# One core, eight blocks: the first FFN of blocks 1 and 2 moved ahead of the attention projections of blocks 0 and 1

## What is computed

```python
x = x + 0.5 * ffn(layernorm(x))             # FFN "1"
x = x + attn(layernorm(x))                  # "A", and within it the gated MLP, "L"
x = x + 0.5 * ffn(layernorm(x))             # FFN "2", same weights as FFN "1"

def ffn(x):   # 8 experts that share wi and wo; each has its own LoRA of rank 4
    top1 = argmax(x @ gate_W.T + gate_b)
    inter = relu(x @ wi_W.T + wi_b + lora[top1](x))        # 256 -> 1024
    return inter @ wo_W.T + wo_b                           # 1024 -> 256

def attn(x):  # 16 heads of 16
    h = rmsnorm(x) * ln1
    q, k, v = h @ wq, h @ wk, h @ wv
    i, f = exp(clip(h @ wi + bi)), sigmoid(h @ wf + bf)
    # state along the 1024 tokens: C = f*C + i * v k^T, n = f*n + i*k ; y = C q / max(|n q|, 1)
    x = x + y @ wo
    h2 = rmsnorm(x) * ln2
    return x + (silu(h2 @ w_gate) * (h2 @ w_up)) @ w_down  # 256 -> 704 -> 256
```

## Time and profile before

| | us |
|---|---|
| median of 3 runs | 936.71 (932.42 to 938.03) |
| span of the profiled execution | 936.9 |
| TensorE busy | 865.0 (92%) |
| VectorE busy | 627.0 (67%) |
| ScalarE busy | 359.0 (38%) |
| GpSimd busy | 244.5 (26%) |
| first FFN matmul of block 0 | 20.06 |
| first gate matmul of block 0's "L" | 175.19 |

### The profile page before, as it was taken

One profiled execution on the slowest core, in us unless ns is written; L12 is line 12 of the kernel. 1 busy time (PEld: TensorE's weight loads), 2 busy tenths in 40 slices (PEclk: granted clock), 3 DMA queues, 4 the chain that ended last, 5 costly groups with the idle time before them and its releaser, 6 DMA issues. The chain is left out here.

```text
span 936.9 us, 30800 instructions
## 1 busy us (share of the span) xinstructions
PE 865.0 (92%) x12744; PEld 823.7 (88%) x12744; DVE 627.0 (67%) x1502; ACT 359.0 (38%) x716; POOL 244.5 (26%) x234
## 2 busy tenths in 40 slices
PE   2958889999899998999899999999989989898998
PEld 2947869999799998999899998999979979898998
DVE  5445677585866858486676758677576787687642
ACT  4453152433533344243523436234343452233431
POOL 2013332320422313322322313332042234411110
PEclk9988999999999999999999999999999999999999
DMA  9105434212243202442133312431035035500000
GB/s 263 57 14 140 131 95 126 66 40 70 83 132 86 58 19 55 124 126 58 36 94 116 87 40 73 139 112 35 24 103 154 11 110 140 152 25 2 1 24 23
DMA packets 66313, 76.04 MB, mean 81 GB/s; under 512 B 12702, under 2 KB 48670, under 8 KB 66176
## 3 DMA queue, kind: packets, MB, share of 16 engines
q1 hardware_dynamic: 66176, 74.09, 28.2%
HBM read 56.75 MB, written 17.30 MB: 79 GB/s over the span
## 5 line engine op out<-in xcount | busy, mean ns | idle before, releaser
L644 ACT ACTIVATE r_h<-bank 128x512 fp32r<-128x512 f32 x128 | 76.5, 598 | 233.6 <-PE bank L1128 164.9
L1093 PE MATMUL bank<-xT_hi,wi_hi 128*128 128x256 f32 x512 | 148.1, 289 | 2.6 <-DVE r_l L836 1.8
L1093 PE MATMUL bank<-wo_hi,r_h 128*128 128x256 f32 x512 | 147.7, 288 | 1.1 <-DVE r_l L836 0.5
L1095 PE MATMUL bank<-xT_lo,wi_hi 128*128 128x256 f32 x512 | 144.1, 282 | 0.0
L1094 PE MATMUL bank<-xT_hi,wi_lo 128*128 128x256 f32 x512 | 144.1, 281 | 0.0
L1095 PE MATMUL bank<-wo_lo,r_h 128*128 128x256 f32 x512 | 143.7, 281 | 0.0
L1094 PE MATMUL bank<-wo_hi,r_l 128*128 128x256 f32 x512 | 143.7, 281 | 0.0
L836 DVE SCALAR_TENSOR_TENSOR r_l<-bank,r_h 128x512 fp32r<-128x512 f32 x128 | 87.9, 687 | 82.7 <-ACT r_h L644 82.1
L1093 PE MATMUL bank<-xT_hi,wgu_hi 128*128 128x256 f32 x352 | 103.1, 293 | 0.6 <-DVE gm L845 0.5
L1093 PEld LDWEIGHTS bank<-xT_hi,wi_hi 128*128 128x128 f32 x512 | 97.3, 190 | 5.0 <-DVE r_l L836 2.4
L1093 PEld LDWEIGHTS bank<-wo_hi,r_h 128*128 128x128 f32 x512 | 96.4, 188 | 3.9 <-issue 2.5
(11 more groups left out here) (157 smaller groups left out, 2143.9 us busy)
## 6 DMA issues: line engine op xcount, KB each, us to landing
dm<-f_scratch SPq DMA_DIRECT2D x128, 128.0 KB, 3.0
arena<-parts_scratch SPq DMA_DIRECT2D x96, 128.0 KB
arena<-parts_scratch SPq DMA_DIRECT2D x96, 64.0 KB
arena<-parts_scratch SPq DMA_DIRECT2D x32, 192.0 KB
x<-in_x SPq DMA_DIRECT2D x16, 256.0 KB, 3.0
parts_scratch<-pa SPq DMA_DIRECT2D x64, 64.0 KB
parts_scratch<-pb SPq DMA_DIRECT2D x64, 64.0 KB
parts_scratch<-pc SPq DMA_DIRECT2D x64, 64.0 KB
```

The source lines that it names most:

```text
L644: nc.scalar.activation(flat(r_h[:, n]), U[use % 2][:], ACT.Relu).then_inc(f_rh, 1)
L1093: nc.tensor.matmul(dst, lh, rh, start=first, stop=False, **more)
L1095: return nc.tensor.matmul(dst, lh, rl, start=False, stop=last, **more)
```

## The change

In the head of the run list two pairs change places: block 1's first FFN stands ahead of block 0's attention, block 2's ahead of block 1's. The rest of the list is the same. All five order strings are replaced, for the whole length of the program. No function changes.

```diff
-RUNS = [("1", 0), ("A", 0), ("1", 1), ("A", 1), ("1", 2)]
+RUNS = [("1", 0), ("1", 1), ("A", 0), ("1", 2), ("A", 1)]
...
 ORDER = {
     "PE": """
-        3G U G 5U V 2U V 2U 2V 4U V U V U 2V 2G 5U G U G 2U G U G 7U V 2U V 2U 2V 4U S U V S Y V 2U M 2V M 2S M 2Y M G 2S Y G 3U M 2U M U M Y S U S G 2Y M U G
+        3G U G 4U V 3U V U V U V G 3U V G 2V U V U G 2V G 5U V 2U V U V 2U V 2U G U V 3U 2V G V 11U 2G Y 2S 3M G Y 2S 2Y 3M U G 2S Y 2M Y 2U Y S 2U V 3U V U 2V
```

More of the change, by code:

```diff
@@ new lines @@
+        M 2V Y U Y 2S 2M Y U M 2U Y V U Y U Y 2V 3M U Y U Y 3U V G 2V G 4U V 2U G V U V G 3U G U V G U V 2U V 3U V 3U V G V 2U V U G 3U V G 2U V G U V U V 4U
+        2V 4U 2V 2U V 2U V 2U 2V""",
+    "DVE": """
+        H 5G 2H G H G 4H 2G R 4H 2G 2R G H 4R H 2G 2R G 2H 2G 4R 2G R 2H G H 3R H G 2R G 4R H R H R 2G R H 2R G H G 4R 2H G R 2D 2Y 2P Y G 3D Y 2P 3Y G Y D 2P
+        Y 2G Y 2R G R D G R P Y G R 2Y 2R Y D R Y G P Y G Y 4R Y R G 3R 2G 2Y 2G 3R G 2R 2G 3R G 4R G D G D 2P 4R G D 2R Y G 4R G Y 4R 4G R Y 2R G P 2R D G 2R
+        2G R Y 3G 2R Y D 4R Y P Y 3R Y D P 2R Y G P R 2Y G Y R G 2R G R Y 2R Y 2D Y G P Y P D 2R G Y P D R Y 2R Y 3G 2R G 5R G 2R 3G 2R G 4R G 3R P Y G 3R G R
+        2Y 2G 2R D 2G R G D R P Y 3R D G P R Y G R 3G 2R G 2R 2Y R 2D 3R Y G P R Y P G Y G 2Y 3R Y 2R Y G 2R G Y D 2R G P D P Y P R Y D Y P R Y R D Y 3G 3R G
+        R D 5R 3G 3R G R G 2R Y R G 4R G 2R G R P G 2Y G 2R 3G 3R P D G 2R D 2G R 2G 2R G D Y 3R P 2R 2Y 2R 2Y R G Y P Y G 2R Y G R 2Y 2R G Y G R D R P G P Y
+        D 2R Y P Y G R Y 2R Y 2G D 2R D R G 3R G 6R G R 3G 3R P 2R G R Y P G 3R G R 2Y 2G 2R G D G R G Y R P Y D G R D 2R P 2G R G 2Y G R D R G D 6R Y R P Y
+        2R 2Y P G Y R Y P G Y 2R G 2R G Y 2R 2G 2Y 2D R P R Y D G R Y R Y R 2G P 2R G Y R D 2R D R Y 2R 3G 3R G Y P G 4R G 3R G 4R 3G 3R 2G R G 2P R G Y G R G
+        R D R Y R G R 2G 2R Y 2R D R Y 2R Y 2R Y G Y P Y G R Y G 2R Y R Y G 2R P G D R Y P G Y R D R G 2Y 2R P Y G R G R G D 3R 2G R G 2R D Y R G 3R Y 2P R D
+        2R G R D 6R P R G Y R G R G R G R G Y R D R G R 2Y P 2R 2Y P G Y D R Y G 2Y R G 2R Y G R P Y R D P 2Y R Y R D 2Y 2G P D R P Y D R 2Y 2G P G R 2Y R D P
+        G Y D R D 2Y D P R Y P R Y 2R 2Y 2G Y 2R Y R D R Y R G R Y 2P R Y 2R Y G R Y 2R Y G R G 4R G R 2G 2R 2G R G 6R G 2R G 4R G 3R 2G 3R 3G 3R G 2R G 2R 2G
+        12R""",
@@ new lines @@
+    "ACT": """
+        6G 2H 2G 10H G R 3H 3R 2G H R 2G H R 2G R 2G R G 4R 4H R H 3G Z 2G R H 2R G R 2H 7R A 2R A G R H A G 2R G R A H 5G Y G Z Y 4R 2G R Z G R Y R 3G 4R Z
+        4R Y A 3R A 3G R 2G A 2R G A 5R 4G R 2G 2R 2G 5R G Z R Z R 4G Z 2R G R G Y 2R G R 2G 3R G 4R A R 2G 2R Y A R A 2G R Z 2R G A R Y 4R Y R G R G R 3G R G
+        5R 2G R 4G 2R 2G 3R G R Y 3R 2G R Z 3G 2R G R 2Z 2R 2G R 2G Z 4R G A G 3R Y 2G A 4R G A Y 3R A 2R Y R 3G 2R 2G 3R G 3R 3G R 3G 2R G R G 2R G 2R Z Y R
+        3G 2R 3G 3R 2G Z G 3R G 4R A 3R 2G Y A 2G 4R A 2Z G Y 4R Y 2R 3G 2R A 2G R G 6R 3G R G R 2G Z 2G 3R G 2R Y R 5G R Z R G 4R 4G 7R A Y 2R A 2G R Z 2G A
+        Y 3R A G 2R Z 2R Y 3R 2G R 3G R G 5R 2G R 4G 2R 2G 3R G 2R Z R 3G R 2G Y Z R G 5R G R 3G 5R A 2R Y 2G A Z 2G 4R Y A G 4R Z A R Y R 4G R G R Z R G 5R Z
+        R 3G 4R G R 2G 3R Y 3R G R A R G 2R 2G A 2G Y R 2G 3R A Z G Z Y 3R Y A 3R 2G Y 3G R 2Z 2R Y G 2R 2Z R Y 3R Y 4R 3G R 3G 3R 3G 2R G R 2G R 2G 4R G 4R
+        2G R 3G R 3G 3R G 8R""",
```

49 lines of the change are left out of this document (15 added, 34 removed).

## The result

The changed kernel takes 956.49 us in the median (952.45 to 958.46), the kernel before 934.96 us on the same chip (932.42 to 938.03). The ratio is 1.022, with a 95% interval of 1.018 to 1.026: slower by about 2%. Forecast was 940 us, no change, in a range of 926 to 955.

The account below looks back on a forecast made before the run. TensorE's work plus its waits was taken to bound the kernel. 936.9 + 2.8 (to the landmark) + 3.0 (block 1's attention start) - 4.0 (later blocks) = 938.7 us, rounded up to 940, range 926 to 955.

Parts of the forecast that it names:

- the landmark: First gate matmul of block 0's gated MLP, at 175.2 us before; forecast at 178.0 us, 2.8 us later.
- (1): Start to block 0's first projection matmul: the 7.0 us of waits are won, and that matmul comes at 77.5 us.
- (2): Block 0's projections: their chain keeps its length, so waits of 4.17 and 1.94 us stay; end at s + 21.2.
- s: Forecast time of block 0's first projection matmul, 77.5 us; later points of the head are counted from it.
- (3): Block 0's last V to first S: stores and loads no longer covered, first S at s + 30, 7.6 us lost.
- (4): Block 0's first two attention tiles, nearly alone, to block 2's first FFN step: 21.5 us, 11.7 of work, 9.8 lost.
- (5): From 129.0 us to the landmark: 40.5 us of work plus 8.5 lost, mostly at block 1's projections.
- (6): Behind the landmark, block 1's first S and state have less work ahead of them: 3 us lost, bounds 0 and 8.
- (7): Later blocks: more cover ahead of projections wins 0.8 us in each of five, -4 us; bounds +4 and -15.
- A: Rival, slower by over 1%: the chain of (3) and (4) is longer than counted, 954 us; chance 0.28.
- B: Rival, faster by over 1%: later blocks decide, with 12 us won around the projections, 928 or 925 us; chance 0.14.
- C: Rival: the early waits go and the new gap of (3) and (4) costs only 6 us, 926 us; chance 0.08.

Follow-up runs that it names:

- k1: Changed kernel with the stacked loads of block 0's second tile issued behind the fourth and fifth `dm` loads; 953.66 us, ratio 1.019.
- k2: Changed kernel with block 0's first-tile stacked loads right behind the `fTz` store, ahead of `cum` store, `dm` and `cumE` loads; 953.42 us, ratio 1.019.
- h2: Kernel before's run list and order up to block 0's gated MLP, then the changed kernel's order; 938.91 us against 934.89, ratio 1.004.
- f4: Changed kernel with block 2's FFN woven through block 0's attention, block 1's first scans, S and query product later; 957.18 us, ratio 1.023.
- f3: Kernel before with only the second swap, block 2's first FFN ahead of block 1's attention; 958.97 us, ratio 1.025.

## Why the prediction was wrong

The chain of the first profile is 8.1 us longer ahead of the landmark than forecast (186.08 for 178.0), and 6.6 behind it (5.6 longer than before, where -1 was forecast).

(1) held. Block 0's first projection matmul came at 77.30 us for 77.5.

(2) held: the last V matmul ended at 98.75, s + 21.4 for s + 21.2, with waits of 4.34 and 2.08 us in the chain. Taking block 1's transposes and gates out of block 0's projections left the chain its length.

(3) is the step that failed in the head, and 5.8 of the 8.1 us are its. "3 us to landing" put the first S at s + 30; it came at s + 36.0 (s + 34.7 in the second profile). SyncE's issues ended 1.3 us later than I had them (s + 28.3), and the stack landed 7.7 us behind its last issue. I had taken the landing of two `dm` loads on an idle queue for that of seven stacked loads behind four `dm` and two `cumE` loads, with the engines at 0.94 to 1.05 of their share. The Trainium skill (DMA: Bandwidth & Descriptors, Anatomy of one DMA) gives a fixed part and a part by bytes, measured on another path; I left out the part by bytes. The seven loads are 768 KB, which at the 176 to 214 GB/s of these rows is 3.7 to 4.5 us, an estimate that would make up the difference; no run tells it from the loads queued ahead. Neither of the two orders of the loads, k1 and k2, shortened the chain.

(4) was right in length: 21.4 us from the first S to the end of block 2's first FFN piece, for 21.5. But TensorE idled only 5.0 of them and was busy for 16.4, at a clock of 0.57, where I had 9.8 lost beside 11.7 at full rate. (5) gave 49.0 us from there to the landmark and it took 51.4, of which the unforeseen wait for `xn` is 3.69. Together: the landmark 10.9 us later where I had 2.8.

(6) and (7): behind the landmark I expected 3 - 4 = -1 us; it is 5.6 longer in the first profile, 6.2 in the second. What neither term had in it are the waits for code: 15.9 and 11.3 us of stalls in the two profiles, 5.9 before, and half clock behind some (the longest, 2.61 us, ends at 378.08). Without the stalls TensorE idles 24.9 us behind the landmark in the kernel before, 25.7 in h2, and 21.4 and 28.5 in the two profiles of the changed kernel. So the gain of (7) isn't seen, and no loss either: its 4 us are within what two executions of one kernel differ by. By moving the blocks' ends the changed kernel was made some 5 us better and the one before 3 to 6 worse.

Two signs of being wrong came in. The idle time behind the landmark is 37.3 us, over the 36 of (7), but the stalls account for the rise. The idle sum is 86.8 us, over the 86 that the prediction as a whole allowed, and the landmark is past 184.

Of the rivals, A had the mechanism in the head, and its time (954 us) is near. That nearness is in part luck: of A's 15 us over the sum the head brought 8.1, and the others came behind the landmark, which A doesn't speak of. Its point (first S later than s + 35) was passed in the first profile and just missed in the second. I gave A 0.28 and wrote against it only that block 2's x is loaded early. B had the later blocks win, and as they are they lost 6 us; C fell with (3). The rule that spoke against the change, the Trainium skill (Perfetto Trace Analysis, Optimization Strategy) on interleaving regimes, pointed the right way: with the FFN back under the round trip TensorE was busy for 21.00 of 21.00 us (f4), and with block 1's projections taken out from under the attention for 9.03 of 21 (f3).

So of the 17 to 21 us some 10 to 11 are the head's, at any of the placings tried. Behind the landmark the pair differs by +6 to about -6 us with the place of the block ends, and what the order of work is worth there can't be read from one pair of runs.

## What to carry to other kernels

A wait that is removed may have lain in the shade of a chain that stays; count the chain, and then ask what covers its far end. Work that can cover is a stock: moved to where nothing waits it is spent, and in the two other placings tried here (f4, f3) it was missing at one round trip or the next. Where TensorE's program has many thousand instructions with runs of tiny matmuls, compare two orders at several shifts of the code, and list the waits that end in "issue", beside the times of the code transfers, before explaining a difference of 1%.

## What was not expected of the hardware

TensorE stalls of 0.4 to 3.0 us recur at the same matmul from run to run, come back on it when 512 instructions are put ahead, and go elsewhere with 150 or 300. All but a few fall into groups of tiny matmuls or just behind them. Each of the 169 ends 1.2 to 1.7 us behind the end of a 16 KB code transfer; the profile's list of waits only says "issue".

A store of the parts took 5.2 to 5.8 us from its issue (93.47, or half a microsecond later for the second of the two) to the point where the wait for it ended (99.23, k2), and seven stacked loads behind six others 7.7 us from the last issue (6.4 in the second profile), where the `dm` loads of the earlier trace rows took 2.8 to 5.0.

The same order with the same idle time cost 7.0 us more busy time behind one head than behind another (730.07 for 723.09): 20.10 us at the lower clock for 3.30.
